# Perceiver block: the cross-partition maximum of the scores moves from TensorE transposes to one GpSimd instruction

## The chip, the cores and the metric

The kernel runs on one core of a Trainium2 chip. The metric is the device time of one execution in microseconds (us); lower is better. Engines are named as in the profile: PE (TensorE matmuls), PEld (its weight loads), DVE (VectorE), ACT (ScalarE), POOL (GpSimd), SP (the queue that issues the DMAs).

## The reference

A block of three residual layers over x of shape (8, 64, 256). The first, a cross attention with 16 heads of 64 over a context of 1601 rows, takes the larger part of the time:

```
xn = layernorm(layernorm(x), gamma, beta)
q  = xn @ w_q ; k, v = split(ctx @ w_kv)
scores = einsum('bqhd,bkhd->bhqk', q * SCALE, k)
attn = softmax(scores, axis=-1)
x = x + (einsum('bhqk,bkhd->bqhd', attn, v) @ w_out + b_out) * tanh(gate)
x = x + linear_attention(layernorm(x))     # 8 heads, 64 tokens
x = x + moe(layernorm(x))                  # 8 experts, top 2, all experts computed
```

The softmax here needs, for each query, the maximum of its scores over the 1601 context rows.

## The kernel before, in words

The weights of the keys are folded into the queries first, so that the scores are `ctx @ qk`, with qk computed once in a prologue, written to a DRAM scratch and read back. All large products are made in three passes of rounded operands: each operand is split into a high part (rounded to fp32r) and a low part (the rest), and hi*hi, hi*lo and lo*hi are summed.

The main loop has NSLOT = 208 slots: NG = 16 groups of SJ = 13 slots. A group is 512 columns (queries times heads of half a batch element), a slot is one piece of 128 context rows (65 rows in the thirteenth). Two groups share one batch element. Every engine has its own program, an unrolled walk over slots (a function `slot` in each), and the engines meet by semaphores. In slot k:

- PE computes the scores of slot k, context rows on the partitions (six matmuls, L1206), into one of two PSUM banks. It waits for `out_ok` and `max_ok` of slot k-2, since the bank must be free. Then it computes p times context of slot k-19 (`times_context`, twelve matmuls, L1224 to L1226).
- ACT copies the scores of slot k-1 out of PSUM (`take_scores`, L668), and takes the exponential and the high part of p of slot k-17 (`exps`, L674 and L677).
- DVE subtracts the maximum (`minus_max`, L882) of slot k-17, makes the low part of p (`low_part`, L907) of slot k-18, and keeps a running elementwise maximum `cmax` over the slots of the group (`running_max`, L890 and L893), in this order.

At the end of a group `cmax` holds 128 partial maxima for each of the 512 columns, and what is needed is their maximum, on every partition (`mbc`). That takes five steps on three engines: PE transposes `cmax` in four blocks (L1262, second slot of the next group), DVE reduces along the row and writes the result out 128 times wide (L899, L902, in `column_max`), PE transposes that back in four blocks (L1272, fourth slot), and ACT copies it to SBUF (L691, `take_max`). The first `minus_max` of the group waits for `mbc_ok`.

The context and qk pieces for later slots are split by POOL. `slot_jobs(k)` lists the pieces of slot k: one context piece for slot k+6 and in four of thirteen slots a piece of qk. Pieces are loaded by SP into a ring `raw` of four buffers (RR = 4); the load of piece n waits until piece n-4 is split (`split_ok`). POOL does both halves: the high part at L578, the low part at L580. In `may_split` it waits for the data and for the target: a score operand (ct) may be overwritten once `scores_ok` is far enough, a piece of the value operand (cn) once `pv_ok` is. Pieces of slots 7 to 19 of each 26 are of the cn kind.

In the sixth to tenth slot of a group (V_U to V_O) the finished sums of the group before are normalised (DVE L917), transposed (PE L1238), multiplied with w_v (PE L1251) and stored (L924). After slot 208 the loop drains while the linear attention of token tiles 0 to 2 (`chain`, with a POOL step `chain_rstd` at L603) starts between its slots. The experts follow.

The lines that the change touches: constants L51 and L54 to L55; buffers `mcol` L214 and `mrow` L252; POOL `split`, `split_job`, `split_pass` (L573 to L598); ACT `take_max` and `slot` (L688 to L712); DVE `column_max` (L895); PE `transpose_u` (L1229), `transpose_max` and `spread_max` (L1256 to L1273) and `slot`.

Of the kernel before, what the change touches and what calls it, by code (L numbers as in the profile page):

```python
# [34 lines left out]
P = 128  # L35
# [14 lines left out]
CNW = 2 * D + 2  # L50
L_SUB, L_LO, L_PV = SJ + 4, SJ + 5, SJ + 6  # L51
PASS = 4 * SJ
NPASS = NSLOT // PASS
V_MT, V_MR, V_MB, V_MC = 1, 2, 3, 3  # L54
V_U, V_UT, V_UTC, V_WV, V_O = 5, 6, 7, 8, 9  # L55
RR = 4
# [57 lines left out]
def build(nc, x, ctx_n, ctx_t, gamma, beta, w_q, w_kt, w_v, w_out, b_out, gate, Wq, Wk, Wv, Wo, bo,  # L114
          W_router, b_router, W1, b1, W2, b2, out):
    with ExitStack() as es:
# [96 lines left out]
        lnT_lo = sb("lnT_lo", [P, DT, TOK], F32R)  # L213
        mcol = sb("mcol", [P, GT])  # L214
        rsum = sb("rsum", [P, GT])
# [35 lines left out]
        pt_lo = lsb("pt_lo", [P, PR, GW], F32R)  # L251
        mrow = lsb("mrow", [P, GT, P])  # L252
        loop_scope.close()
# [32 lines left out]
        pool_step = sem("pool_step")  # L286
        split_hi = sem("split_hi")
        ones_ok = sem("ones_ok")
        split_ok = sem("split_ok")
# [16 lines left out]
        max_ok = sem("max_ok")  # L306
        mt_ok = sem("mt_ok")
        mcol_ok = sem("mcol_ok")
        mrow_ok = sem("mrow_ok")
        mb_ok = sem("mb_ok")  # L310
        mbc_ok = sem("mbc_ok")
# [238 lines left out]
        def _(pool):  # L550
# [21 lines left out]

            def split(src, hi, lo, hi_count, done):  # L573

                z = zero[0:src.shape[0], :]
                for _ in range(len(src.shape) - 2):
                    z = z.unsqueeze(1)
                pool.tensor_tensor(hi, src, z.broadcast_to(tuple(src.shape)), ALU.add).then_inc(split_hi, 1)  # L578
                pool.wait_ge(split_hi, hi_count + 1)
                pool.tensor_tensor(lo, src, hi.bitcast(F32), ALU.subtract).then_inc(done, 1)  # L580

            def split_job(job, i):

                no = linear(i, lambda q: JOB_NO[shift(job, q)])
                may_split(pool, job, i)
                split(*split_views(job, i), no, split_ok)

            def split_pass(i, of):
                for u in range(PASS):
                    for job in slot_jobs(of * PASS + u):  # L590
                        split_job(shift(job, -of), i)

            for job in FIRST_JOBS:
                split_job(job, 0)
            split_pass(0, 0)
            with pool.Fori(0, NPASS - 2) as i:
                split_pass(i, 1)
            split_pass(NPASS - 1, NPASS - 1)  # L598

            def chain_rstd(m, which):  # L600
# [25 lines left out]
        def _(act):  # L626
# [60 lines left out]

            def take_max(i, u):  # L688

                act.wait_ge(mb_ok, linear(i, lambda q: q * (PASS // SJ) + u // SJ))  # L690
                act.activation(mbc[:, (u // SJ - 1) % 2, :], wps[:, 1, :], ACT.Copy).then_inc(mbc_ok, 1)  # L691

            def slot(i, u, k):

                if 1 <= k <= NSLOT:
                    take_scores(i, u - 1)
                if u % SJ == V_MC and SJ <= k < NSLOT + SJ:
                    take_max(i, u)
                if L_SUB <= k < NSLOT + L_SUB:
                    exps(i, u - L_SUB)  # L700
                if u % SJ == V_UTC and k >= 2 * SJ:
                    take_ut(i, u)

            for u in range(PASS):
                slot(0, u, u)
                if u in LATE_TILE:
                    take_qk(LATE_TILE[u])
                if u - 1 in LATE_TILE:
                    first_high(LATE_TILE[u - 1])
            with act.Fori(0, NPASS - 1) as i:  # L710
                for u in range(PASS):
                    slot(i, u, PASS + u)  # L712
            def chain(m, o):

# [100 lines left out]
        def _(dve):  # L815
# [78 lines left out]

            def column_max(i, u):  # L895

                g = linear(i, lambda q: q * (PASS // SJ) + u // SJ)
                dve.wait_ge(mt_ok, g)
                dve.tensor_reduce(mcol[:], wps[:, 0, :].rearrange("p (t q) -> p t q", q=P), AX.X,  # L899
                                  ALU.max).then_inc(mcol_ok, 1)  # L900
                dve.wait_ge(mcol_ok, g)
                dve.tensor_copy(mrow[:], mcol[:].unsqueeze(2).broadcast_to((P, GT, P))).then_inc(mrow_ok, 1)  # L902

            def low_part(i, u):
# [22 lines left out]
            def slot(i, u, k):  # L927
                if L_SUB <= k < NSLOT + L_SUB:
                    minus_max(i, u - L_SUB)
                if L_LO <= k < NSLOT + L_LO:  # L930
                    low_part(i, u - L_LO)
                if 1 <= k <= NSLOT:
                    running_max(i, u - 1)
                if u % SJ == V_MR and SJ <= k < NSLOT + SJ:
                    column_max(i, u)
                if u % SJ == V_U and k >= 2 * SJ:
                    take_u(i, u)
                if u % SJ == V_O and k >= 2 * SJ:
                    b = u // (2 * SJ) - 1
                    if isinstance(i, int):  # L940
                        take_o(i, u, slice((i * 2 + b) * Q, (i * 2 + b + 1) * Q))
                    else:
                        take_o(i, u, bass.ds(i * (2 * Q) + (b + 2) * Q, Q))
# [198 lines left out]
        def _(pe):  # L1142
# [86 lines left out]
            def transpose_u(i, u):  # L1229
                for x in range(2):  # L1230
# [3 lines left out]
                    else:  # L1234
                        pe.wait_ge(mbc_ok, linear(i, lambda q: min(q * (PASS // SJ) + u // SJ, NG)))
                    for a in range(2):
# [18 lines left out]

            def transpose_max(i, u):  # L1256

                pe.wait_ge(max_ok, linear(i, lambda q: q * PASS + u // SJ * SJ))
                if not isinstance(i, int) or i > 0 or u >= 3 * SJ:
                    pe.wait_ge(o_ok, linear(i, lambda q: q * (PASS // SJ) + u // SJ - 2))  # L1260
                for t in range(GT):
                    ins = pe.transpose(wps[:, 0, t * P:(t + 1) * P],  # L1262
                                       cmax[:, (u // SJ - 1) % 2, t * P:(t + 1) * P], ident[:])
                ins.then_inc(mt_ok, 1)

            def spread_max(i, u):

                pe.wait_ge(mrow_ok, linear(i, lambda q: q * (PASS // SJ) + u // SJ))
                if not isinstance(i, int) or i > 0 or u >= 3 * SJ:
                    pe.wait_ge(utc_ok, linear(i, lambda q: (q * (PASS // SJ) + u // SJ - 2) * 2))  # L1270
                for t in range(GT):
                    ins = pe.transpose(wps[:, 1, t * P:(t + 1) * P], mrow[:, t, :], ident[:])  # L1272
                ins.then_inc(mb_ok, 1)  # L1273

            def slot(i, u, k):
                if k < NSLOT:
                    scores(i, u)
                if u % SJ == V_MT and SJ <= k < NSLOT + SJ:
                    transpose_max(i, u)
                if u % SJ == V_MB and SJ <= k < NSLOT + SJ:  # L1280
                    spread_max(i, u)
                if L_PV <= k < NSLOT + L_PV:
# [263 lines left out]
```

## Time and profile before

| | before |
|---|---|
| median of 3 runs | 981.15 us (978.63 to 981.46) |
| the profiled execution, time | 980.75 us |
| its span, first to last instruction | 979.0 us |
| PE busy | 936.0 us (96%) |
| DVE busy | 738.2 us (75%) |
| POOL busy | 561.9 us (57%) |
| ACT busy | 503.1 us (51%) |
| granted TensorE clock, mean | 0.991 |

Busy shares are averages over stages. Matmuls are pipelined and the profile models their ends, so that a PE matmul's duration is longer than the distance to the next one; distances between starts tell what an instruction costs. The loop runs from about 35 us to 737 us of the span.

### The profile page before, as it was taken

Reading aid. Unit: us, or ns where it says so; the run is one execution under the profiler, and the core shown is the slowest. Engines: PE = TensorE matmul, PEld = TensorE weight load, DVE = VectorE, ACT = ScalarE, POOL = GpSimd, SP = SyncE. Lnnn points to the kernel's source line nnn. Section 1 sums busy time; section 2 is a strip of 40 time slices with the busy share of each in tenths; the row PEclk is TensorE's granted clock in tenths of the full one; section 3 lists DMA queues with packets and bytes.
Section 4 is the critical chain, followed back from the end, with each engine's and each line's share of the span. In section 5 each row is a group of like instructions: output and inputs, shape, how many; then the busy total and the mean of one; then the engine's idle time right before and its main releaser. Section 6 shows DMA issues by size and latency. Waiting matters only on the chain.

```text
span 979.0 us, 18047 instructions
## 1 busy us (share of the span) xinstructions
PE 936.0 (96%) x5988; PEld 805.1 (82%) x5988; DVE 738.2 (75%) x1151; ACT 503.1 (51%) x856; POOL 561.9 (57%) x593
## 2 busy tenths in 40 slices
PE   6999999999999999999999999999998799999998
PEld 3568888888888888888889888888886587888887
DVE  4659778787877977878787797775875667888776
ACT  2557656566565665656646566564442333344332
POOL 5729779678948957967894895610010442444540
PEclk9999999999999999999999999999999799999999
DMA  5872122212211212221221221101005022222200
GB/s 161 271 253 55 51 60 63 53 45 62 63 38 58 66 36 60 62 52 46 60 67 30 58 70 37 51 1 65 1 1 172 5 84 86 87 86 86 86 1 22
DMA packets 75083, 66.40 MB, mean 68 GB/s; under 512 B 7920, under 2 KB 71680, under 8 KB 75008
## 3 DMA queue, kind: packets, MB, share of 16 engines
q1 hardware_dynamic: 75008, 65.37, 22.3%
q8 instruction: 51, 0.84, 0.3%
q14 instruction: 24, 0.20, 0.1%
HBM read 57.48 MB, written 7.86 MB: 67 GB/s over the span
## 4 chain that ended last, share of the span: by engine, by line
PE 85%; DVE 10%; ACT 2%; issue 2%; POOL 1%; DMA 0%; SPq 0%; DVEq 0%; ACTq 0%; POOLq 0%
PE sps L1206 27%; PE scp L1224 9%; PE scp L1226 9%; PE scp L1225 9%; PE scp L1416 5%; PE sps L1402 5%; PE wps L1402 4%; PE scp L1417 3%; DVE u_sb L917 2%; PE wps L1251 2%; DVE st L882 1%; PE sps L1160 1%; PE sps L1319 1%; PE scp L1174 1%; PE sps L1339 1%
## 5 line engine op out<-in xcount | busy, mean ns | idle before, releaser
L1224 PE MATMUL scp<-cn,pt_hi 128*128 128x258 f32 (+1 forms) x832 | 239.2, 288 | 3.6 <-DVE pt_lo L907 2.8
L1225 PE MATMUL scp<-cn,pt_hi 128*128 128x256 f32 (+1 forms) x832 | 234.9, 282 | 0.0
L1226 PE MATMUL scp<-cn,pt_lo 128*128 128x258 f32 (+1 forms) x832 | 234.8, 282 | 0.0
L907 DVE TENSOR_TENSOR pt_lo<-st,pt_hi 128x512 fp32r<-128x512 f32 (+1 forms) x208 | 196.6, 945 | 6.8 <-ACT pt_hi L677 6.8
L668 ACT ACTIVATE st<-sps 128x512 f32<-128x512 f32 (+1 forms) x208 | 123.6, 594 | 148.4 <-PE sps L1206 147.7
L882 DVE TENSOR_TENSOR st<-st,mbc 128x512 f32<-128x512 f32 (+1 forms) x208 | 158.9, 764 | 38.6 <-ACT mbc L691 38.0
L1206 PE MATMUL sps<-qk_hi,ct_hi 128*128 128x512 f32 (+1 forms) x416 | 168.3, 405 | 12.6 <-DVE cmax L893 5.6
L674 ACT ACTIVATE st<-st 128x512 f32<-128x512 f32 (+1 forms) x208 | 130.2, 626 | 88.7 <-DVE st L882 88.2
L1224 PEld LDWEIGHTS scp<-cn,pt_hi 128*128 128x128 f32 (+1 forms) x832 | 156.9, 189 | 13.7 <-DVE pt_lo L907 5.7
L1206 PE MATMUL sps<-qk_hi,ct_lo 128*128 128x512 f32 (+1 forms) x416 | 164.2, 395 | 0.0
L1206 PE MATMUL sps<-qk_lo,ct_hi 128*128 128x512 f32 (+1 forms) x416 | 163.4, 393 | 0.0
L1225 PEld LDWEIGHTS scp<-cn,pt_hi 128*128 128x128 f32 (+1 forms) x832 | 157.2, 189 | 7.4 <-issue 0.2
L1226 PEld LDWEIGHTS scp<-cn,pt_lo 128*128 128x128 f32 (+1 forms) x832 | 157.7, 190 | 0.0
L893 DVE TENSOR_TENSOR cmax<-cmax,sps 128x512 f32<-128x512 f32 x192 | 130.7, 681 | 33.9 <-ACT st L668 32.8
L578 POOL TENSOR_TENSOR cn<-raw,zero 128x256 fp32r<-128x256 f32 (+1 forms) x104 | 80.2, 772 | 120.4 <-PE scp L1226 113.9
L677 ACT ACTIVATE pt_hi<-st 128x512 fp32r<-128x512 f32 (+1 forms) x208 | 131.7, 633 | 7.5
L580 POOL TENSOR_TENSOR cn<-raw,cn 128x256 fp32r<-128x256 f32 (+1 forms) x104 | 100.3, 964 | 8.1
L1206 PEld LDWEIGHTS sps<-qk_hi,ct_hi 128*128 128x128 f32 (+1 forms) x416 | 76.5, 184 | 32.8 <-issue 14.2
L580 POOL TENSOR_TENSOR ct_lo<-raw,ct_hi 128x256 fp32r<-128x256 f32 (+1 forms) x104 | 96.0, 923 | 8.2
L578 POOL TENSOR_TENSOR ct_hi<-raw,zero 128x256 fp32r<-128x256 f32 (+1 forms) x104 | 88.3, 849 | 11.1 <-DMA raw<-ctx_t 11.1
L1206 PEld LDWEIGHTS sps<-qk_hi,ct_lo 128*128 128x128 f32 (+1 forms) x416 | 76.4, 184 | 20.3
L1206 PEld LDWEIGHTS sps<-qk_lo,ct_hi 128*128 128x128 f32 (+1 forms) x416 | 76.6, 184 | 10.3
(212 smaller groups left out, 1460.7 us busy)
## 6 DMA issues: line engine op xcount, KB each, us to landing
w_raw<-W SPq DMA_DIRECT2D x16, 1024.0 KB, 7.6
raw<-ctx_t SPq DMA_DIRECT2D x96, 128.0 KB, 2.2
raw<-ctx_n SPq DMA_DIRECT2D x96, 128.0 KB, 2.0
raw<-qk_scratch SPq DMA_DIRECT2D x56, 128.0 KB, 2.0
qk_scratch<-stage_b SPq DMA_DIRECT2D x4, 896.0 KB, 4.7
qk_scratch<-stage_a SPq DMA_DIRECT2D x4, 896.0 KB, 4.5
wq_sb<-w_q SPq DMA_DIRECT2D x1, 1024.0 KB, 5.0
wkt_sb<-w_kt SPq DMA_DIRECT2D x1, 1024.0 KB, 7.9
```

What stands on the lines that cost most here:

```text
L578: pool.tensor_tensor(hi, src, z.broadcast_to(tuple(src.shape)), ALU.add).then_inc(split_hi, 1)
L580: pool.tensor_tensor(lo, src, hi.bitcast(F32), ALU.subtract).then_inc(done, 1)
L668: act.activation(st[0:rows(j), par, j, :], sps[0:rows(j), u % 2, :], ACT.Copy).then_inc(out_ok, 1)
L674: act.activation(p, p, ACT.Exp).then_inc(exp_ok, 1)
L677: act.activation(pt_hi[0:rows(j), r, :], p, ACT.Copy).then_inc(hi_ok, 1)
L882: dve.tensor_tensor(p, p, mbc[0:rows(j), par, :], ALU.subtract).then_inc(sub_ok, 1)
L893: dve.tensor_tensor(m, m, src, ALU.max).then_inc(max_ok, 1)
L907: dve.tensor_tensor(pt_lo[0:rows(j), r, :], st[0:rows(j), par, j, :], pt_hi[0:rows(j), r, :].bitcast(F32), ALU.subtract).then_inc(lo_ok, 1)
L1206: ins = pe.matmul(sps[0:rows(j), u % 2, :], a[:, dt, cols], v[:, par, dt, :], start=c == 0, stop=c == 5)
L1224: pe.matmul(scp[:, t, 0:D + 2], hi, cn[0:rows(j), j, 0:D + 2], start=j == 0, stop=False)
L1225: pe.matmul(scp[:, t, 0:D], hi, cn[0:rows(j), j, D + 2:CNW], start=False, stop=False)
L1226: ins = pe.matmul(scp[:, t, 0:D + 2], lo, cn[0:rows(j), j, 0:D + 2], start=False, stop=j == SJ - 1)
```

## The change

Four edits that belong together:

1. POOL computes `mbc` from `cmax` by one `partition_all_reduce` with max for each group (`all_max`), with a small instruction ahead of it that carries the touch of `cmax`. It stands in POOL's program at the first slot of the next group, ahead of that slot's pieces, and after the last piece for the last group. The transposes on PE, `column_max` on DVE and `take_max` on ACT are gone.
2. In the loop ACT makes the high part of every piece (`high_part`, at the end of its slot k for the pieces of slot k), and POOL only the low part, after a wait for `slot_hi`. The 26 pieces ahead of the loop stay wholly with POOL.
3. L_SUB, L_LO and L_PV grow by one: `minus_max` is done for slot k-18, p times context for slot k-20. V_U to V_O move along by one, and so does the start of the last chain.
4. The second half of `transpose_u` waits for the copies of the group before (`utc_ok`), where it waited for `mbc_ok`.

```diff
-L_SUB, L_LO, L_PV = SJ + 4, SJ + 5, SJ + 6
+L_SUB, L_LO, L_PV = SJ + 5, SJ + 6, SJ + 7
-V_MT, V_MR, V_MB, V_MC = 1, 2, 3, 3
-V_U, V_UT, V_UTC, V_WV, V_O = 5, 6, 7, 8, 9
+V_U, V_UT, V_UTC, V_WV, V_O = 6, 7, 8, 9, 10
...
-            def split(src, hi, lo, hi_count, done):
+            def split(src, hi, lo, hi_count, done, both):
...
+                if both:
...
+                else:
+                    pool.wait_ge(slot_hi, hi_count + 1 - len(FIRST_JOBS))
                 pool.tensor_tensor(lo, src, hi.bitcast(F32), ALU.subtract).then_inc(done, 1)
...
+            def all_max(g, par):
+
+                pool.wait_ge(max_ok, (g + 1) * SJ)
+                pool.tensor_tensor(mtouch[:], cmax[:, par, 0:1], zero[:], ALU.add)
+                pool.partition_all_reduce(mbc[:, par, :], cmax[:, par, :], P, bass.bass_isa.ReduceOp.max)\
+                    .then_inc(mbc_ok, 1)
 
             def split_pass(i, of):
                 for u in range(PASS):
+                    if u % SJ == 0 and not (of == 0 and u == 0):
+                        all_max(linear(i, lambda q: q * (PASS // SJ) + u // SJ - 1), (u // SJ - 1) % 2)
                     for job in slot_jobs(of * PASS + u):
-                        split_job(shift(job, -of), i)
+                        split_job(shift(job, -of), i, False)
...
+            all_max(NG - 1, (NG - 1) % 2)
...
-            def take_max(i, u):
...
+            def high_part(job, i):
+
+                src, hi, _ = split_views(job, i)
+                may_split(act, job, i)
+                act.activation(hi, src, ACT.Copy).then_inc(slot_hi, 1)
+
+            def split_slot(i, of, u):
+
+                for job in slot_jobs(of * PASS + u):
+                    high_part(shift(job, -of), i)
...
             for u in range(PASS):
                 slot(0, u, u)
+                split_slot(0, 0, u)
...
-            def column_max(i, u):
...
-                        pe.wait_ge(mbc_ok, linear(i, lambda q: min(q * (PASS // SJ) + u // SJ, NG)))
+                        wait(pe, utc_ok, linear(i, lambda q: (q * (PASS // SJ) + u // SJ - 2) * 2))
...
-            def transpose_max(i, u):
...
-            def spread_max(i, u):
```

## Rows read from the trace of the kernel before

**Rows 1.** Page, busy time by engine, and the granted clock in 40 slices
```profile
PE 936.0 (96%) x5988; PEld 805.1 (82%) x5988; DVE 738.2 (75%) x1151; ACT 503.1 (51%) x856; POOL 561.9 (57%) x593
...
PEclk9999999999999999999999999999999799999999
```

**Rows 2.** Page, chain of work that ended last, share by engine
```profile
PE 85%; DVE 10%; ACT 2%; issue 2%; POOL 1%; DMA 0%; SPq 0%; DVEq 0%; ACTq 0%; POOLq 0%
```

**Rows 3.** Timeline of PE: start us, duration us, engine, line, operation, tiles
```profile
384.29 0.60 PE L1262 MATMUL wps<-ident,cmax 128*128 128x128 f32 x4
...
384.84 0.28 PE L1225 MATMUL scp<-cn,pt_hi 128*128 128x256 f32 x1
...
390.41 0.60 PE L1272 MATMUL wps<-ident,mrow 128*128 128x128 f32 x4
...
390.96 0.28 PE L1225 MATMUL scp<-cn,pt_hi 128*128 128x256 f32 x1
...
392.29 0.39 PE L1206 MATMUL sps<-qk_hi,ct_hi 128*128 128x512 f32 x1
...
393.67 0.28 PE L1224 MATMUL scp<-cn,pt_hi 128*128 128x258 f32 x1
393.79 0.28 PE L1225 MATMUL scp<-cn,pt_hi 128*128 128x256 f32 x1
...
395.10 0.40 PE L1206 MATMUL sps<-qk_hi,ct_hi 128*128 128x512 f32 x1
```

**Rows 4.** Groups by line: out<-in, shapes, count, busy us, mean ns, idle before
```profile
L899 DVE TENSOR_REDUCE mcol<-wps 128x4 f32<-128x512 f32 x16 | 10.9, 684 | 0.0
L1272 PE MATMUL wps<-ident,mrow 128*128 128x128 f32 x64 | 9.6, 272 | 0.7 <-DVE mrow L902 0.7
L691 ACT ACTIVATE mbc<-wps 128x512 f32<-128x512 f32 x16 | 9.6, 598 | 39.7 <-PE wps L1272 39.7
L674 ACT ACTIVATE st<-st 128x512 f32<-128x512 f32 (+1 forms) x208 | 130.2, 626 | 88.7 <-DVE st L882 88.2
L668 ACT ACTIVATE st<-sps 128x512 f32<-128x512 f32 (+1 forms) x208 | 123.6, 594 | 148.4 <-PE sps L1206 147.7
```

**Rows 5.** Timeline of PE in the filling of the loop
```profile
72.52 0.47 PE L1206 MATMUL sps<-qk_hi,ct_hi 128*128 128x512 f32 x1 [0.78 <-DVE cmax L893]
...
75.56 0.47 PE L1206 MATMUL sps<-qk_hi,ct_hi 128*128 128x512 f32 x1 [1.40 <-DVE cmax L893]
...
78.49 0.39 PE L1206 MATMUL sps<-qk_hi,ct_hi 128*128 128x512 f32 x1
```

**Rows 6.** Timeline of POOL, the first qk piece
```profile
72.76 0.70 POOL L578 TENSOR_TENSOR qk_hi<-raw,zero 128x256 fp32r<-128x256 f32 x1 [15.95 <-DMA raw<-qk_scratch]
```

**Rows 7.** Timeline of ACT, a rounding of a 128x256 piece
```profile
40.72 0.42 ACT L648 ACTIVATE qk_hi<-stage_b 128x256 fp32r<-128x256 f32 x1
```

**Rows 8.** Groups by line, POOL's elementwise work
```profile
L580 POOL TENSOR_TENSOR cn<-raw,cn 128x256 fp32r<-128x256 f32 (+1 forms) x104 | 100.3, 964 | 8.1
L609 POOL TENSOR_TENSOR w_lo<-w_raw,w_hi 128x1024 fp32r<-128x1024 f32 x16 | 40.5, 2536 | 70.0 <-ACT w_hi L763 70.0
```

**Rows 9.** Timeline of DVE around the end of a group
```profile
420.32 0.68 DVE L893 TENSOR_TENSOR cmax<-cmax,sps 65x512 f32<-65x512 f32 x1
...
432.61 0.69 DVE L882 TENSOR_TENSOR st<-st,mbc 128x512 f32<-128x512 f32 x1 [2.65 <-ACT mbc L691]
```

**Rows 10.** Timeline of PE, first score matmul after that group's end
```profile
420.94 0.39 PE L1206 MATMUL sps<-qk_hi,ct_hi 128*128 128x512 f32 x1
```

**Rows 11.** DMA issues: size and median us to landing
```profile
raw<-ctx_n SPq DMA_DIRECT2D x96, 128.0 KB, 2.0
```

**Rows 12.** Timeline of DVE, low part beside an idle and a busy POOL
```profile
394.88 0.68 DVE L907 TENSOR_TENSOR pt_lo<-st,pt_hi 128x512 fp32r<-128x512 f32 x1
...
400.72 1.17 DVE L907 TENSOR_TENSOR pt_lo<-st,pt_hi 128x512 fp32r<-128x512 f32 x1
```

**Rows 13.** Timeline of PE, the idle time after the transposes of u
```profile
402.63 0.47 PE L1206 MATMUL sps<-qk_hi,ct_hi 128*128 128x512 f32 x1 [0.81 <-ACT st L668]
```

More of the change, by code:

```diff
@@ L213, in build @@
         lnT_lo = sb("lnT_lo", [P, DT, TOK], F32R)
-        mcol = sb("mcol", [P, GT])
+        mtouch = sb("mtouch", [P, 1])
         rsum = sb("rsum", [P, GT])
@@ L251, in build @@
         pt_lo = lsb("pt_lo", [P, PR, GW], F32R)
-        mrow = lsb("mrow", [P, GT, P])
         loop_scope.close()
@@ L287, in build @@
         split_hi = sem("split_hi")
+        slot_hi = sem("slot_hi")
         ones_ok = sem("ones_ok")
@@ L306, in build @@
         max_ok = sem("max_ok")
[L307 to L310, printed above, removed]
         mbc_ok = sem("mbc_ok")
@@ L571, in _, with split_job @@
             pool.wait_ge(mask_ok, 1)
-            def split(src, hi, lo, hi_count, done):
[L575 to L579, printed above, removed]
+            def split(src, hi, lo, hi_count, done, both):
+                if both:
+                    z = zero[0:src.shape[0], :]
+                    for _ in range(len(src.shape) - 2):
+                        z = z.unsqueeze(1)
+                    pool.tensor_tensor(hi, src, z.broadcast_to(tuple(src.shape)), ALU.add).then_inc(split_hi, 1)
+                    pool.wait_ge(split_hi, hi_count + 1)
+                else:
+                    pool.wait_ge(slot_hi, hi_count + 1 - len(FIRST_JOBS))
                 pool.tensor_tensor(lo, src, hi.bitcast(F32), ALU.subtract).then_inc(done, 1)
-            def split_job(job, i):
+            def split_job(job, i, both):
                 no = linear(i, lambda q: JOB_NO[shift(job, q)])
-                may_split(pool, job, i)
-                split(*split_views(job, i), no, split_ok)
+                if both:
+                    may_split(pool, job, i)
+                split(*split_views(job, i), no, split_ok, both)
+            def all_max(g, par):
[3 more added lines that the diff above has]
+                    .then_inc(mbc_ok, 1)
             def split_pass(i, of):
                 for u in range(PASS):
+                    if u % SJ == 0 and not (of == 0 and u == 0):
+                        all_max(linear(i, lambda q: q * (PASS // SJ) + u // SJ - 1), (u // SJ - 1) % 2)
                     for job in slot_jobs(of * PASS + u):
-                        split_job(shift(job, -of), i)
+                        split_job(shift(job, -of), i, False)
             for job in FIRST_JOBS:
-                split_job(job, 0)
+                split_job(job, 0, True)
             split_pass(0, 0)
@@ L686, in take_ut @@
                                    wps[:, x, :].rearrange("p (a t q) -> p a t q", a=2, t=DT), ACT.Copy).then_inc(utc_ok, 1)
-            def take_max(i, u):
-                act.wait_ge(mb_ok, linear(i, lambda q: q * (PASS // SJ) + u // SJ))
-                act.activation(mbc[:, (u // SJ - 1) % 2, :], wps[:, 1, :], ACT.Copy).then_inc(mbc_ok, 1)
+            def high_part(job, i):
[5 more added lines that the diff above has]
+                    high_part(shift(job, -of), i)
             def slot(i, u, k):
@@ L696, in slot @@
                     take_scores(i, u - 1)
-                if u % SJ == V_MC and SJ <= k < NSLOT + SJ:
-                    take_max(i, u)
                 if L_SUB <= k < NSLOT + L_SUB:
@@ L709, in _ @@
                     first_high(LATE_TILE[u - 1])
-            with act.Fori(0, NPASS - 1) as i:
+            with act.Fori(0, NPASS - 2) as i:
                 for u in range(PASS):
                     slot(i, u, PASS + u)
+                    split_slot(i, 1, u)
+            for u in range(PASS):
+                slot(NPASS - 1, u, PASS * (NPASS - 1) + u)
+                split_slot(NPASS - 1, NPASS - 1, u)
             def chain(m, o):
@@ L893, in running_max @@
                     dve.tensor_tensor(m, m, src, ALU.max).then_inc(max_ok, 1)
-            def column_max(i, u):
[L897 to L902, printed above, removed]
             def low_part(i, u):
@@ L933, in slot @@
                     running_max(i, u - 1)
-                if u % SJ == V_MR and SJ <= k < NSLOT + SJ:
-                    column_max(i, u)
                 if u % SJ == V_U and k >= 2 * SJ:
@@ L1254, in times_wv @@
                 ins.then_inc(wv_ok, 1)
-            def transpose_max(i, u):
[L1258 to L1264, printed above, removed]
-            def spread_max(i, u):
[L1268 to L1273, printed above, removed]
             def slot(i, u, k):
@@ L1277, in slot @@
                     scores(i, u)
[L1278 to L1281, printed above, removed]
                 if L_PV <= k < NSLOT + L_PV:
```

## The prediction

> **What bounds the kernel now.** I read the page first: PE is busy 96% of the span at full clock [rows 1], and the chain of work that ended last runs over PE for 85% of it, over DVE for 10% and over POOL for 1% [rows 2]. So an instruction taken from PE is worth its whole distance, and one taken from DVE or ACT only where PE waited for it. The timeline of PE gives the beat: the scores of successive slots start at 392.29 and 395.10 us, so a slot is 2.81 us, and PE stands nowhere inside it [rows 3]. A group is 13 slots, 36.6 us, plus what PE does once per group.
>
> **What is removed.** Between the last score matmul and the second context matmul of an ordinary slot PE has 393.79 - 393.67 = 0.12 us from first to second; with the transposes of `cmax` it goes from 384.29 to 384.84, 0.55 us, and with those of `mrow` from 390.41 to 390.96, again 0.55 us [rows 3]. Each of the two is thus worth 0.43 us, and 16 groups have both: 32 x 0.43 = 13.8 us off PE. DVE loses its reduction of 0.68 us and the wide copy per group, and ACT 0.60 us [rows 4]. PE waited for that chain for 0.7 us only, once, in the drain [rows 4], so this counts as nothing: the cover is the slack between the ready `cmax` and the first `minus_max`.
>
> **What is moved.** ACT takes 182 context and 56 qk roundings at 0.42 us [rows 7], 100 us over 208 slots, 0.48 us a slot. Its slot was the copy of scores, 0.59, the exponential, 0.63 [rows 4], and a rounding taken as long as that, 1.85 us, and becomes 2.3 us against the beat of 2.81: no cost, as long as it does not wait. POOL's share per piece falls to the low part, 0.96 us [rows 8], 17 pieces in most groups, some 16 us of 40. No DMA is added, but SP's loads still wait for POOL's `split_ok` of four pieces earlier, and now ACT, in order, waits for those loads. What is queued behind ACT's wait is the next copy of scores, which DVE's running maximum and through it PE's scores two slots on need. Two costs come of that.
>
> The filling of the loop. The first qk piece is there at 72.76 us [rows 6], since SP first waits for the scratch and issues the weights. POOL alone waited before. Now ACT stands at the end of its slot 14 until then: rounding 0.42 [rows 7], copy of scores 14 0.59 [rows 4], running maximum 0.68 [rows 9], PE starts the scores of slot 16 at 74.5. Slots without a context product cost 1.6 us (1.39 of scores, and a bank that comes free late), so slot 20 starts at 80.9, against 78.49 [rows 5]: 2.4 us late. It started then with one context product done, 1.43 us, which is now still to do, and the 0.86 us of transposes are counted as gained above though they are inside the 78.49. The filling costs 2.4 + 1.4 + 0.9 = 4.7 us. The two idle times of 0.78 and 1.40 us there [rows 5] are in this balance.
>
> The steady loop is the size of the reduction against a deadline, below. The extra slot of latency gives DVE one more beat, and moves the drain by one slot, in which PE has the chains to work on: 0, within 1.5 us either way. In the drain the step at L603 is queued behind the last `all_max` on POOL; the first token tile's statistics come some 7 us after the last maximum, so up to that a reduction hides.
>
> **The price of the reduction, T.** No row shows one. From below: POOL's subtraction of 128x1024 takes 2.54 us [rows 8], so one pass over 128x512 is 1.27 us. From above: 128 partitions one after the other, 128 passes, 163 us. A tree of halvings has seven levels: one pass each is 8.9 us, a move and a maximum each 17.8 us. I take four passes, 5.1 us: nearest to the row, as the instruction reads once, folds, spreads and writes once, on an engine whose passes take all partitions together. This is the weak term of the sum.
>
> **The deadline.** Let slot 13 start at 0. After groups whose last slots carry ct pieces the maximum ends as now, at 420.32 + 0.68 = 421.00, beside a slot 13 starting at 420.94 [rows 9, 10]: at 0.1. In the other groups ACT rounds the cn pieces of slots 7 to 19, which are free only when the context product of the same slot is done, that is at the next slot's start; then 0.42 + 0.59 + 0.68 us make the maximum end at 1.7. POOL reduces until 1.7 + T and touches no piece meanwhile. The ring holds four pieces: those of slots 13, 14 (two) and 15. ACT's piece of slot 16 is loaded when POOL has done the piece of slot 13 (0.96 [rows 8]), with 2.0 us of DMA [rows 11]; then 0.42 rounding, 0.59 copy of scores 16, 0.68 maximum, and PE wants to start the scores of slot 18 at 5 x 2.81 = 14.1. So 1.7 + T + 0.96 + 2.0 + 0.42 + 0.59 + 0.68 <= 14.1: T up to 7.7 us is free after these eight groups and up to 9.3 after the other eight. `minus_max` itself allows more: it could wait now until 432.61, 11.6 us after the maximum [rows 9], and gets a beat more. Each us beyond costs 1 us per group.
>
> **Sum.** With T = 5.1: 980.75 - 13.8 + 4.7 = 971.7 us for the profiled execution. That execution lies 0.4 us under the median, so I forecast 972. Contention is set at nothing: the low part on DVE takes 0.68 us with POOL still and 1.17 with POOL working [rows 12], and the 0.81 us idle after the transposes of u [rows 13] (some eight such places, their causes on DVE and ACT) could shrink with POOL's second half gone: up to 5 us of gain. If the reduction itself disturbs DVE the same way, it takes the same back. Ends 966 and 976 for this case.
>
> [...]
>
> **The rivals.**
> 1. *The ring of four turns the reduction into a wait (slower).* Place: ACT's rounding in the fourth slot of a group, waiting for a load that waits for POOL. It decides from T = 7.7 us. With the seven levels of 8.9 us: 8 x 1.2 = 10 us back, 981. With 12 us: 8 x 4.3 + 8 x 2.7 = 56 less 9.1, 1028. With 17.8 us: 8 x 10.1 + 8 x 8.5 = 149 less 9.1, 1121. For it: POOL's rows are all slow beside DVE's, and nothing in the trace shows that it crosses partitions cheaply. Against: seven passes are needed before it costs anything. It equals no change at T of about 8.5 to 9.2.
> 2. *The reduction walks (much slower).* POOL folds partition by partition, 16 to 128 passes of 1.27 us, 20 to 163 us a group: 16 x (T - 8.5) less 9.1, from 1,156 to 3,440 us. For it: no row excludes it. Against: each elementwise row has all partitions at once. [...]
> 3. *The gain does not come out.* PE loses its transposes and waits instead for DVE at the same places, because ACT now delivers the scores up to 1.7 us later in half of the slots. For it: PE's waits name DVE and ACT [rows 5, 13]. Against: the running maximum of a cn slot ends 1.7 us after the next slot's start and is wanted at 2.81. It would give 978 to 984.
>
> **How the numbers follow.** Forecast case 0.52 (966 to 976). Rival 1 beyond no change 0.29, mostly 984 to 1121; rival 3, with the edge of rival 1, 0.07; rival 2 0.12. A measurement of this kernel can tell about 0.3%, 3 us, from no change. Faster: the forecast case and a little of the edge, 0.54; the same 0.05; slower 0.41. The range reaches down to 965 (all the contention gone) and up to 1055, where T is just under 14 us: at 14, 8 x 6.3 + 8 x 4.7 - 9.1 = 79 more, 1060. Above that lie the rest of rival 1 and rival 2, under 0.2 together. The forecast case has its own range, 966 to 976.
>
> **What would show it.** In the profile after: the mean duration of POOL's reduction in the groups by line, the one number on which all turns; PE 13 to 14 us less busy in the window of the loop; slots 14 to 16 of the filling with an idle time of about 5 us on PE, behind ACT; ACT at about 590 us busy. If the longest waits of ACT are those of the rounding for `raw` loads, one per group and each growing with T, rival 1 holds. If DVE's wait for `mbc` is the longest instead, my deadline is misplaced. The prediction is wrong if T is over 8 us, or if PE's loop keeps its length with T under 7.

## The result and the profile after

| | before | after |
|---|---|---|
| median | 981.17 us | 1107.74 us (1106.28 to 1109.88, 4 runs) |
| ratio, 95% interval | | 1.13 (1.1281 to 1.132) |
| the profiled execution, time | 980.75 us | 1109.88 us |
| its span | 979.0 us | 1108.1 us |
| granted TensorE clock, mean | 0.991 | 0.938 |

The change is 127 us slower. The forecast was 972 and the range ended at 1055. The page of the kernel after, busy time and clock, and the shares of the chain that ended last, which answer to [rows 1, 2]:

```profile
PE 963.0 (87%) x5860; PEld 824.0 (74%) x5860; DVE 671.3 (61%) x1119; ACT 562.9 (51%) x1078; POOL 349.2 (32%) x387
...
PEclk9989898998989899898989889898899998999999
...
PE 43%; issue 33%; POOL 10%; DVE 7%; DMA 2%; ACT 2%; SPq 1%; POOLq 0%; DVEq 0%; ACTq 0%
```

PE has its 128 transposes fewer and is still busy for 27 us longer, at 87% of the span; the granted clock has fallen, which is taken up below. No engine has taken over: POOL is at 32%. A third of the chain is "issue", time in which the engine waited for nothing that the profile shows. The chain of waits says where:

```profile
PE sps L1214 <- DVE cmax L912: 106.1, 31, 8.1
POOL mbc L591 <- issue: 101.1, 16, 10.5
...
ACT ct_hi L701 <- DMA raw<-ctx_t: 66.7, 7, 10.2
...
ACT cn L701 <- DMA raw<-ctx_n: 62.5, 7, 9.9
...
POOL ct_lo L578 <- issue: 49.0, 7, 7.5
POOL cn L578 <- issue: 48.6, 7, 7.1
```

PE waits for the running maximum, ACT waits for pieces in `raw` (14 times, 9 to 10 us, the last 6.6), and POOL stands 6.3 us on the mean ahead of each of 16 reductions and 7 us behind each. The timeline of POOL after one group shows one of them:

```profile
444.91 0.57 POOL L590 TENSOR_TENSOR mtouch<-cmax,zero 128x1 f32<-128x1 f32 x1 [0.56 <-DVE cmax L912]
451.31 1.80 POOL L591 PARTITION_ALL_REDUCE mbc<-cmax  x1 [5.82 <-issue]
459.86 1.31 POOL L578 TENSOR_TENSOR cn<-raw,cn 128x256 fp32r<-128x256 f32 x2 [6.75 <-issue]
```

And the queries on the two lines show what was issued there (count, shortest/median/longest ns, first and last start):

```profile
L591 POOLq MODIFY_POOL_CONFIG  x32: 3/6/8, 64.5 to 783.1; - x32
L591 POOL PARTITION_ALL_REDUCE mbc<-cmax x16: 1802/1842/2305, 75.0 to 790.2; - x16
...
L578 POOLq MODIFY_POOL_CONFIG  x30: 98/98/98, 76.7 to 744.6; - x30
```

The reduction itself is recorded at 1.84 us, far below the 5.1 us that the prediction took. But two MODIFY_POOL_CONFIG are issued ahead of each reduction, and two ahead of the first subtraction behind it. No line of the kernel asks for them. They stand where POOL goes from `tensor_tensor` to `partition_all_reduce` and where it goes back: 16 times there (x32) and 16 times back (x30, and x2 ahead of the step at L612 in the drain, at 792.2 us). I call such a pair a change of library, after the call `load_library`, which puts one into reload_pair below. The trace has a wait at every one of them: 5.82 us ahead of the reduction above, 5.8 to 6.2 us in the loop behind the first, which has 10.46, and 6.7 to 7.5 us behind a reduction. From the touch at 444.91 to the first low part at 459.86 POOL is away for 14.95 us, of which 1.8 us are the work. The rest of this text calls that the absence.

### The profile page after: what moved, and what is told of

It is laid out like the page before. It is cut to its first block, busy times and chain, and to the rows that moved or that the text cites. A ratio compares the mean times of both kernels' runs of the same rounds, so it can differ in the third digit from the quotient of the medians.

```text
span 1108.1 us, 17700 instructions
## 1 busy us (share of the span) xinstructions
PE 963.0 (87%) x5860; PEld 824.0 (74%) x5860; DVE 671.3 (61%) x1119; ACT 562.9 (51%) x1078; POOL 349.2 (32%) x387
## 4 chain that ended last, share of the span: by engine, by line
PE 43%; issue 33%; POOL 10%; DVE 7%; DMA 2%; ACT 2%; SPq 1%; POOLq 0%; DVEq 0%; ACTq 0%
PE sps L1214 10%; PE scp L1401 4%; PE wps L1387 4%; PE sps L1387 4%; PE scp L1232 3%; PE scp L1234 3%; PE scp L1233 3%; POOL ct_lo L578 3%; POOL cn L578 3%; PE scp L1402 2%; POOL qk_lo L578 2%; POOL mbc L591 2%; DVE cmax L912 1%; DVE u_sb L927 1%; ACT st L677 1%
## 5 line engine op out<-in xcount | busy, mean ns | idle before, releaser
L1214 PE MATMUL sps<-qk_hi,ct_hi 128*128 128x512 f32 (+1 forms) x416 | 179.6, 432 | 107.6 <-DVE cmax L912 106.1
L1232 PEld LDWEIGHTS scp<-cn,pt_hi 128*128 128x128 f32 (+1 forms) x832 | 164.5, 198 | 16.2 <-DVE pt_lo L917 5.7
L1214 PE MATMUL sps<-qk_hi,ct_lo 128*128 128x512 f32 (+1 forms) x416 | 172.1, 414 | 0.0
L1214 PE MATMUL sps<-qk_lo,ct_hi 128*128 128x512 f32 (+1 forms) x416 | 172.0, 414 | 0.0
L1233 PEld LDWEIGHTS scp<-cn,pt_hi 128*128 128x128 f32 (+1 forms) x832 | 164.2, 197 | 9.4 <-issue 0.5
L917 DVE TENSOR_TENSOR pt_lo<-st,pt_hi 128x512 fp32r<-128x512 f32 (+1 forms) x208 | 152.4, 733 | 1.5 <-ACT pt_hi L686 1.5
L901 DVE TENSOR_TENSOR st<-st,mbc 128x512 f32<-128x512 f32 (+1 forms) x208 | 150.7, 724 | 0.6 <-ACT tg L792 0.6
L578 POOL TENSOR_TENSOR cn<-raw,cn 128x256 fp32r<-128x256 f32 (+1 forms) x104 | 77.1, 744 | 223.3 <-ACT cn L701 173.7
L578 POOL TENSOR_TENSOR ct_lo<-raw,ct_hi 128x256 fp32r<-128x256 f32 (+1 forms) x104 | 85.4, 823 | 139.6 <-ACT ct_hi L701 89.5
L701 ACT ACTIVATE cn<-raw 128x256 fp32r<-128x256 f32 (+1 forms) x91 | 37.8, 415 | 127.8 <-PE scp L1234 65.3
L1401 PE MATMUL scp<-w_sp,h_hi 128*128 128x512 f32 x224 | 79.8, 397 | 1.0 <-DVE h_lo L1122 1.0
```

The source lines that it names most:

```text
L901: dve.tensor_tensor(p, p, mbc[0:rows(j), par, :], ALU.subtract).then_inc(sub_ok, 1)
L917: dve.tensor_tensor(pt_lo[0:rows(j), r, :], st[0:rows(j), par, j, :], pt_hi[0:rows(j), r, :].bitcast(F32), ALU.subtract).then_inc(lo_ok, 1)
L1214: ins = pe.matmul(sps[0:rows(j), u % 2, :], a[:, dt, cols], v[:, par, dt, :], start=c == 0, stop=c == 5)
L1232: pe.matmul(scp[:, t, 0:D + 2], hi, cn[0:rows(j), j, 0:D + 2], start=j == 0, stop=False)
L1233: pe.matmul(scp[:, t, 0:D], hi, cn[0:rows(j), j, D + 2:CNW], start=False, stop=False)
L1401: pe.matmul(scp[:, m, :], h_hi[:, f, ms], w2_sp[:, s, f, :], start=f == 0, stop=False)
```

## The experiments

The theory, A: the loss is POOL's absence, through the ring of four buffers, by the deadline of the prediction. The rivals: the reduction hides work that its record does not show (C); the rounding on ACT or the later slot cost much (B); the ring does not matter and only the first subtraction waits.

**One elementwise pass in place of the reduction.**

```diff
-                pool.tensor_tensor(mtouch[:], cmax[:, par, 0:1], zero[:], ALU.add)
-                pool.partition_all_reduce(mbc[:, par, :], cmax[:, par, :], P, bass.bass_isa.ReduceOp.max).then_inc(mbc_ok, 1)
+                pool.tensor_tensor(mbc[:, par, :], cmax[:, par, :], zero[:].broadcast_to((P, GW)), ALU.add).then_inc(mbc_ok, 1)
```

> The changed kernel with the reduction and its touch replaced by one elementwise POOL pass of 128x512 (maxima of each partition alone, so the output is not the reference's); nothing needs another POOL library. Theory A (the loss is POOL's absence of 15 us per group: a library load of 5.9 us, the reduction of 1.8 us, a load back of 6.8 us): with 1.3 us of absence all of it goes, and the sum of the prediction for a short reduction holds, 972 us (966 to 976). Rival B (the rounding on ACT and the later slot cost much by themselves): it stays above 990.

Measured: 968.14 us, ratio 0.9863 (0.9829 to 0.9898); the profiled execution 971.09 us, where the prediction's sum says 971.7. PE is busy 926.0 us of a span of 969.3. Its timeline in the filling of the loop has the one long wait:

```profile
73.89 0.77 PE L1212 MATMUL sps<-qk_hi,ct_hi 128*128 128x512 f32 x1 [5.86 <-DVE cmax L910]
```

All the other edits of the change are in this kernel, so B falls: together with the loss of the transposes they gain. The whole loss is in what was replaced. Its four runs are two pairs, 965.2 us at a granted clock of 0.994 and 971.1 to 971.3 us at 0.987 and 0.989; the median lies between them, so differences of medians against it are good to some 3 us.

**The changes of library without the reduction.** A call of `load_library` stands ahead of the same elementwise pass.

```diff
+                pool.load_library(library_config.all_libraries[1])
```

(behind the touch, ahead of the pass of one_pass)

> The changed kernel with the reduction replaced by one elementwise pass, and the two library loads kept ahead of it (the reduction is left out). Theory A: POOL is away for about 0.6 + 13 + 1.3 = 15 us as in the changed kernel, so 1095 to 1115 us though nothing is reduced across partitions. Rival C (the reduction itself, or work of it that the record of 1.8 us does not show, takes the time): below 1000.

Measured: 1098.73 us, ratio 1.1211 (1.1191 to 1.123), 131 us over one_pass, with nothing reduced. The queries on the line of the call, L592, and on that of the pass behind it, L593, have two MODIFY_POOL_CONFIG a group on each:

```profile
L592 POOLq MODIFY_POOL_CONFIG  x32: 4/6/8, 64.6 to 770.1; - x32
```

```profile
L593 POOLq MODIFY_POOL_CONFIG  x32: 7/7/7, 73.9 to 777.7; - x32
```

The timeline of its POOL after one group:

```profile
440.07 0.57 POOL L591 TENSOR_TENSOR mtouch<-cmax,zero 128x1 f32<-128x1 f32 x1 [0.56 <-DVE cmax L913]
453.56 1.03 POOL L593 TENSOR_TENSOR mbc<-cmax,zero 128x512 f32<-128x512 f32 x1 [12.92 <-issue]
```

And the timeline of its ACT behind it:

```profile
457.54 0.42 ACT L702 ACTIVATE cn<-raw 128x256 fp32r<-128x256 f32 x1 [8.61 <-DMA raw<-ctx_n]
```

A change there and back is 12.92 us of idle POOL, and T, from the touch to the first low part, 14.5 us. C falls: the 6.75 us behind the reduction in the kernel after belong to the change of library, not to a hidden tail.

**Is it the ring? Five, seven and ten passes.** The same pass repeated, each waiting for the one before, and no library change: POOL is away for as long as I choose.

```diff
+                pool.wait_ge(pass_ok, g * 9 + 1)
+                pool.tensor_tensor(mbc[:, par, :], cmax[:, par, :], zero[:].broadcast_to((P, GW)), ALU.add).then_inc(pass_ok, 1)
...
```

> As one_pass, with ten elementwise passes in a row, 12.5 us of POOL per group and no library load. If the deadline of the ring is right (7.7 us after half of the groups, 9.3 after the others): 8 x 4.8 + 8 x 3.2 = 64 us more than one_pass, about 1036. If instead only the first subtraction of the group sets the deadline (about 14.9 us after the maximum), the same as one_pass.

> As one_pass, with five passes in a row; a pass took 1.04 to 1.45 us from start to start in ten_passes, so POOL is away for 6 to 7 us per group. Deadline of the prediction (7.7 and 9.3 us): free, the same as one_pass, 968 (965 to 972). If the deadline lies lower than I reckon, it is over 975.

> As one_pass, with seven passes in a row, 9 to 10 us of POOL per group. Deadline of the prediction: at 10 us 8 x 2.3 + 8 x 0.7 = 24 us more than one_pass, 992 (at 9 us 978), and up to 20 us above that if PE's clock falls after each wait, as it did with ten passes. If only the first subtraction sets the deadline: 968.

The expected times were 968 us for five passes, 992 us for seven (up to 20 us more with the clock) and 1036 us for ten. The absence T is read on POOL's timeline, from the start of the first pass to the end of the last. Of seven passes:

```profile
444.94 1.42 POOL L591 TENSOR_TENSOR mbc<-cmax,zero 128x512 f32<-128x512 f32 x1 [1.16 <-DVE cmax L923]
...
453.68 1.97 POOL L603 TENSOR_TENSOR mbc<-cmax,zero 128x512 f32<-128x512 f32 x1
```

Of ten passes:

```profile
437.28 1.42 POOL L591 TENSOR_TENSOR mbc<-cmax,zero 128x512 f32<-128x512 f32 x1 [0.56 <-DVE cmax L929]
...
450.45 1.04 POOL L609 TENSOR_TENSOR mbc<-cmax,zero 128x512 f32<-128x512 f32 x1
```

| kernel | T, us | by the deadlines 7.7 and 9.3, over one_pass | measured median | over one_pass | PE's wait for `cmax` in all | PE busy |
|---|---|---|---|---|---|---|
| one_pass | 1.4 | 0 | 968.14 | | 12.1 | 926.0 |
| five_passes | 7.4 | 0 | 971.21 | 3 | 12.6 | 925.8 |
| seven_passes | 10.7 | 24 + 11 = 35 | 1011.73 | 44 | 39.8 | 934.9 |
| ten_passes | 14.2 | 52 + 39 = 91 | 1079.08 | 111 | 86.8 | 959.1 |
| reload_pair | 14.5 | 54 + 42 = 96 | 1098.73 | 131 | 95.2 | 959.9 |
| the change | 14.95 | 58 + 45 = 103 | 1107.74 | 140 | 106.1 | 963.0 |

Up to 7.4 us hardly anything happens; at 10.7 us the loss is 44 us. The rival that only the first subtraction matters (968 in every row) falls. PE's timeline shows the two deadlines one by one. The waits at 288.31 and 331.18 are of seven_passes, those at 215.46 and 360.08 of ten_passes, in each the wait behind a ct piece first, then that behind a cn piece:

```profile
288.31 0.47 PE L1225 MATMUL sps<-qk_hi,ct_hi 128*128 128x512 f32 x1 [1.36 <-DVE cmax L923]
331.18 0.47 PE L1225 MATMUL sps<-qk_hi,ct_hi 128*128 128x512 f32 x1 [3.27 <-DVE cmax L923]
```

```profile
215.46 0.77 PE L1231 MATMUL sps<-qk_hi,ct_hi 128*128 128x512 f32 x1 [4.87 <-DVE cmax L929]
360.08 0.76 PE L1231 MATMUL sps<-qk_hi,ct_hi 128*128 128x512 f32 x1 [6.70 <-DVE cmax L929]
```

With T = 10.7 the deadlines 9.3 and 7.7 give waits of 1.4 and 3.0 us; PE's are 1.3 to 1.5 and 3.0 to 3.3, six of each, in turn. With 14.2 they give 4.9 and 6.5; PE's are 4.3 to 4.9 and 6.4 to 6.7, apart from two of 3.4 late in the loop. But the ring makes PE wait behind 14 of the 16 groups only (behind 12 of them by more than 1 us with seven passes): the first falls into the filling, and behind the last no piece comes.

The expected time for seven passes was low because their T is 10.7 us and not the 9 to 10 that I wrote, and that for ten passes because theirs is 14.2 and not 12.5: in these loops a pass takes 1.37 to 1.97 us beside a working DVE, and 1.04 alone. The ratios are 0.989 (0.9865 to 0.9914), 1.0329 (1.0289 to 1.0368) and 1.0999 (1.098 to 1.1019).

The measured steps are 9, 20 and 37 us larger than the deadline gives for seven passes, ten passes and the change. PE's longer work at the lower clock makes the difference, while the waits alone are no more than the deadline gives. In the profiled executions the scores of slot 207, the last of the loop, start 42.3, 110.5 and 128.6 us later than in one_pass. 27.7, 74.7 and 94.0 us of this are waits for `cmax`. Up to that point PE runs the same matmuls, and is busy with them for 14.0, 35.6 and 35.4 us longer (641.8, 663.4 and 663.2 us against 627.8), at a mean granted clock of 0.98, 0.94 and 0.93 against 0.99. Behind the loop the change loses another 10.2 us, which the passes do not. 7.8 us of this are one wait in the drain, behind the last change of library:

```profile
POOL rstd L612 <- issue: 6.9, 1, 6.9
DVE ln_out L989 <- POOL rstd L612: 9.8, 2, 9.1
PE sps L1310 <- DVE ln_out L989: 7.8, 1, 7.8
```

In the kernel after, the timeline of PE around one wait:

```profile
455.42 0.39 PE L1214 MATMUL sps<-qk_hi,ct_lo 128*128 128x512 f32 x1
464.45 0.76 PE L1214 MATMUL sps<-qk_hi,ct_hi 128*128 128x512 f32 x1 [7.19 <-DVE cmax L912]
465.02 0.63 PE L1214 MATMUL sps<-qk_lo,ct_hi 128*128 128x512 f32 x1
465.44 0.63 PE L1214 MATMUL sps<-qk_hi,ct_lo 128*128 128x512 f32 x1
...
469.27 0.39 PE L1214 MATMUL sps<-qk_hi,ct_hi 128*128 128x512 f32 x1
469.51 0.39 PE L1214 MATMUL sps<-qk_lo,ct_hi 128*128 128x512 f32 x1
```

And the windows before, in and behind it (columns: window, length, busy us and instructions of PE, PEld, DVE, ACT, POOL, granted clock, DMA share, GB/s):

```profile
440.00:455.00 15.00, 15.00 (x97) 13.30 (x96) 10.99 (x17) 10.59 (x21) 3.75 (x4) 1.00 0.11 33
455.00:463.00 8.00, 2.27 (x16) 1.93 (x14) 0.00 (x0) 0.31 (x1) 2.67 (x4) 0.93 0.11 34
463.00:470.00 7.00, 5.54 (x22) 4.86 (x23) 3.95 (x6) 4.44 (x11) 2.29 (x3) 0.59 0.32 87
```

PE comes back slow from 7.19 us of idle: the matmuls of the scores start 0.43 us apart, and 0.24 us apart again by 469.27. The granted clock is 0.59 from 463 to 470 us; ahead of the wait, from 440 to 455, it was 1.00. Six matmuls of scores take 2.7 us in place of 1.4, and the twelve products behind them 2.1 in place of 1.4: 2.0 us for this wait, and 35.4 / 14 = 2.5 us on the mean.

**Edits 2 and 3 alone, on the kernel before.**

> The kernel before with edit 2 alone: ACT rounds the pieces of the loop, POOL makes the low parts; the maximum by transposes and the slot distances as before. Theory A: only the filling costs, 4.7 us less the 0.9 us of transposes that the sum had put in it, so 985; less some us if POOL's smaller share frees DVE. Rival B (ACT's waits for the context product of the same slot cost in every group): over 990.

> Edits 2 and 3 without the reduction: ACT rounds, and everything after the maximum is one slot later. Theory A: within 3 us of act_only, so 982 to 988. If the later slot costs one slot of products at the drain in full, 2.8 us more.

> The kernel before with edit 3 alone, every step after the maximum one slot later. Theory A: within 1.5 us of before, 980 to 983, as PE has the chains to do in the drain. Faster than before by 2 to 3 us if the extra beat removes idle times of PE behind DVE; act_and_later came out 3 us under act_only.

The first is edit 2 alone, the second edits 2 and 3, the third edit 3 alone, all with the transposes as before:

```diff
+            def split_slot(i, of, u):
+
+                for job in slot_jobs(of * PASS + u):
+                    high_part(shift(job, -of), i)
...
+                else:
+                    pool.wait_ge(slot_hi, hi_count + 1 - len(FIRST_JOBS))
```

```diff
-L_SUB, L_LO, L_PV = SJ + 4, SJ + 5, SJ + 6
+L_SUB, L_LO, L_PV = SJ + 5, SJ + 6, SJ + 7
...
-V_U, V_UT, V_UTC, V_WV, V_O = 5, 6, 7, 8, 9
+V_U, V_UT, V_UTC, V_WV, V_O = 6, 7, 8, 9, 10
```

Measured: act_only 984.7 us, ratio 1.003 (1.0018 to 1.0043); act_and_later 981.57 us, 1.0009 (0.9992 to 1.0026); later_only 978.0 us, 0.997 (0.9949 to 0.9991). The rounding on ACT costs 3.6 us. The extra slot lowers the median by 3.1 us in both places where it was added, where the theory gave 980 to 983 for later_only and 982 to 988 for act_and_later. It is not shown that the extra beat of DVE does this. At the same granted clock the gain is all but gone: later_only's profiled execution and that of before, both at 0.991, are 979.62 and 980.75, and act_and_later takes 984.4 to 986.0 at 0.987 and 0.988, where act_only has 982.8 to 985.0. What differs is how often a run has the higher clock: 0.991 or less in 3 of 10 runs of later_only and in 9 of 13 of before beside it. Why that is so stays open.

**Repair: no elementwise work for POOL in the loop.** The low parts go to DVE, one slot behind ACT's high parts; POOL has only the sixteen reductions in the loop, without the touch and written out so that their waits are constants.

```diff
+            def low_split(i, of, u):
+                for job in slot_jobs(of * PASS + u):
...
+                    dve.wait_ge(slot_hi, no)
+                    dve.tensor_tensor(lo, src, hi.bitcast(F32), ALU.subtract).then_inc(split_ok, 1)
```

> The changed kernel with the low parts of the pieces moved from POOL to DVE, so that POOL has nothing but the sixteen reductions in the loop and its library is loaded once. Theory A: POOL's reduction then takes 1.8 us and hides, and PE keeps the 13.8 us; DVE goes from 3 x 0.68 us a slot to that and 1.3 x 0.43 = 2.6 us, with 0.15 us a slot for the sums of a finished group, just under the beat of 2.81, so 970 to 985. If DVE becomes the bound it shows as PE idle behind cmax in every group: up to 1000.

Measured: 974.99 us, ratio 0.9949 (0.993 to 0.9969). The query on its reduction:

```profile
L590 POOL PARTITION_ALL_REDUCE mbc<-cmax x16: 1784/3092/3094, 64.9 to 659.8; - x16
L590 POOLq MODIFY_POOL_CONFIG  x2: 3/3/3, 56.7 to 56.8; - x2
```

Only one change of library is left for the sixteen reductions, ahead of the first, at 56.7 us, where POOL was idle anyway, and the loop is free of the 15 us. But the kernel is 6.8 us slower than one_pass: DVE has the low parts of 0.42 us each and is busy 727.7 us, against 673.7. PE's waits for the maximum, from the list of waits of one_pass, then of this kernel (total, times, longest):

```profile
PE sps L1212 <- DVE cmax L910: 12.1, 17, 5.9
```

```profile
PE sps L1230 <- DVE cmax L907: 16.8, 20, 6.2
```

Outside the filling the wait for the running maximum grows from 6.2 to 10.6 us; that this is the maximum standing behind the low parts in DVE's queue is the likely reason, and no run shows it alone. In exchange a low part of p takes 0.68 us on the mean [rows 12]. The profiled executions lie only 3.9 us apart, which these waits cover; the 6.8 us between the medians hold the scatter of both with the clock (low_on_dve ran from 972.2 us at 0.994 to 979.7 us at 0.987).

**Repair of the filling.** What makes ACT wait there is the first qk piece, which stands behind the issues of the weights in SP's queue. Here `load_pass` issues them eight slots later; their first use is after the loop.

```diff
-                    if of == 0 and u == SJ:
+                    if of == 0 and u == SJ + 8:
                         load_weights()
```

> low_on_dve with SP's ten loads of tail weights moved behind the first qk and context pieces (from slot 13 to slot 21). In low_on_dve PE stands 6.2 us in the filling behind ACT, which waits for the first qk piece. If that piece is late because SP issues the weights first, the stall goes and 5 to 6 us come back: 969 to 970. If the piece waits for the scratch itself, nothing changes: 975.

Measured: 969.25 us, ratio 0.986 (0.983 to 0.989), 5.7 us less, as expected. PE's longest wait in the filling, in its timeline, first in low_on_dve and then here:

```profile
74.58 0.76 PE L1230 MATMUL sps<-qk_hi,ct_hi 128*128 128x512 f32 x1 [6.16 <-DVE cmax L907]
```

```profile
76.01 0.47 PE L1231 MATMUL sps<-qk_hi,ct_hi 128*128 128x512 f32 x1 [1.57 <-DVE cmax L908]
```

On PE's timeline the scores of slot 39 start at 132.65 us in place of 140.53, 7.9 us earlier. Of this 3.8 us are left at the end of the profiled executions: from 655 to 800 us the granted clock is 0.94 here and 0.98 in low_on_dve. Of the three repaired kernels with the true maximum, this is the fastest: 11.9 us under the kernel before and 138 under the change.

**The extra slot once more.** The same kernel with edit 3 undone (`minus_max` back at k-17):

> low_dve_weights_later with edit 3 undone as well: the subtraction again 17 slots behind, the context product 19. The reduction lasts 1.8 to 3.1 us in low_on_dve, so its result is there before the subtraction one slot earlier wants it, and the pieces of the value operand come free one slot earlier for ACT. Theory A: the same or up to 2 us faster than low_dve_weights_later. Rival: DVE, at 2.7 us a slot, needs the extra beat, and it is 3 to 10 us slower.

Measured: 975.29 us, ratio 0.9944 (0.9925 to 0.9963), 6 us slower: the rival of the expectation holds and its theory does not. Here the slot of latency is worth 6 us, and the loop itself shows it: from the scores of slot 39 to those of slot 195 it takes 485.7 us against 479.5. PE's waits for `cmax` are 16.0 us against 10.7. On the kernel before, with DVE free of the low parts of the pieces, the same stretch gained 0.4 us by it (488.8 against 489.2).

## Why the prediction was wrong

**The step that failed is "The price of the reduction, T".** It asked what the instruction works, bounded the passes by rows and took 5.1 us. The work is 1.84 us, less than half. What counts is the time for which POOL is away, and that is 14.95 us: two changes of library a group, 5.8 us ahead and 6.75 behind, which reload_pair shows without any reduction (12.92 us, +131 us). The sum had no term for them. I did not ask what POOL runs between two reductions: subtractions, and in the trace of the kernel after each of the sixteen reductions, and what POOL runs first behind each, has its own two MODIFY_POOL_CONFIG and its own wait. No row of before could show it: its trace has no MODIFY_POOL_CONFIG but the two at 1.4 us. With T = 14.95 the prediction's own formula adds 8 x 7.25 + 8 x 5.65 = 103 us to 971.7: 1075, already outside the range, which stopped at a T of 14.

**The deadline was right**, and closely: waits of 3.0 to 3.3 and 1.3 to 1.5 us at T = 10.7, where 7.7 and 9.3 give 3.0 and 1.4. The mechanism is rival 1 as written, at its place: fourteen waits of ACT for `raw`, 9 to 10 us each and the last 6.6, where I had named "one per group and each growing with T". That is two groups fewer than the formula counts. The 103 us of the formula, 90 for fourteen groups, meet 101.8 us more of idle PE only because the 94.0 us of waits have the 7.8 us of the drain beside them. There the prediction let a reduction of up to 7 us hide ahead of the step at L603; POOL was away for longer than that.

**The price beyond the deadline was too low.** 1 us per us per group gives 91 of the 111 us of ten passes and 103 of 140 of the change. It leaves out that PE returns slow from 7.19 us of idle (0.59 granted over the next 7 us), 35.4 us in the loop of the change. The clock of [rows 1] is full but for one slice, and the sum had no term for it.

**The transposes: right.** From act_and_later (981.57) to one_pass (968.14) they and their chain go and one pass of POOL comes: 13.4 us, against 13.8 [rows 3]. What left DVE and ACT [rows 4] was rightly counted at next to nothing: from the scores of slot 39 to those of slot 195 the step is 11.2 us, and 12 x 0.86 = 10.3 of them are the transposes.

**The rest of the sum: two wrong terms that nearly cancel.** One_pass took 971.09 us where the sum says 971.7, and act_only 984.7 where 985 was expected. Both hits are in part luck: in one_pass the filling cost 2.5 us more than its term, and the loop 4.0 us less than the beat of before, as the starts of the scores of slots 39 and 195 show (PE's timeline, six score matmuls to a slot), before, then act_only, then one_pass:

```profile
135.61 0.39 PE L1206 MATMUL sps<-qk_hi,ct_hi 128*128 128x512 f32 x1
...
624.79 0.39 PE L1206 MATMUL sps<-qk_hi,ct_hi 128*128 128x512 f32 x1
```

```profile
143.38 0.39 PE L1228 MATMUL sps<-qk_hi,ct_hi 128*128 128x512 f32 x1
...
628.57 0.39 PE L1228 MATMUL sps<-qk_hi,ct_hi 128*128 128x512 f32 x1
```

```profile
139.63 0.39 PE L1212 MATMUL sps<-qk_hi,ct_hi 128*128 128x512 f32 x1
...
614.49 0.39 PE L1212 MATMUL sps<-qk_hi,ct_hi 128*128 128x512 f32 x1
```

**The filling: right in place, too small in size.** PE waits 5.86 us behind `cmax` where about 5 were expected, and the scores of slot 16 start at 73.89 (forecast 74.5). But at slot 39 act_only is 7.8 us late where 3.8 were reckoned. One_pass is 4.0 us late with two groups' transposes (1.7 us) gone and one product (1.4 us) still to do, so 7.2 us where the sum has 4.7. A part is the clock again: in one_pass the granted clock is 0.99 from 60 to 71 us and 0.53 from 71 to 78 us (in before 1.00 in both), and the scores of slots 16 and 17 take 2.7 and 1.9 us. The first qk piece behind the weights in SP's queue [rows 6] is the cause: with the weights later slot 39 starts 7.9 us earlier.

**ACT's rounding in the loop: not at nothing, but a gain.** From slot 39 to slot 195, twelve groups, before takes 489.2 us and act_only, with the same transposes, 485.2: 4.0 us less. One_pass takes 474.9, which is 14.3 less, and 10.3 of these are the transposes. The prediction had named this and set it at nothing: up to 5 us in PE's idle times like that of [rows 13], "with POOL's second half gone". They are gone in act_only (list of waits, before, then act_only):

```profile
PE sps L1206 <- ACT st L668: 4.9, 6, 0.8
```

```profile
PE sps L1228 <- ACT st L673: 0.9, 1, 0.9
```

ACT's roundings took 0.40 to 0.42 us as in [rows 7], but pieces in a row start 0.31 us apart; ACT was busy 562.9 us, not 590.

**The later slot: 0 within 1.5** fits the profiled execution, 1.1 us less at the same clock; the median of later_only is 3.2 us lower, with the open cause told above.

The low part of p falls from 0.95 us on the mean (median 1.10) to 0.73 after, and to 0.68 in low_on_dve [rows 12]. The query on the low part, before and after (shortest/median/longest ns):

```profile
L907 DVE TENSOR_TENSOR pt_lo<-st,pt_hi x208: 674/1097/1229, 74.1 to 734.5; 128x512 fp32r<-128x512 f32 x96, 65x512 fp32r<-65x512 f32 x8
```

```profile
L917 DVE TENSOR_TENSOR pt_lo<-st,pt_hi x208: 676/683/1606, 82.7 to 865.2; 128x512 fp32r<-128x512 f32 x96, 65x512 fp32r<-65x512 f32 x8
```

**The other rivals.** The walk (rival 2) falls: 1.84 us for 128 partitions. That the gain does not come out (rival 3, 978 to 984) falls with one_pass. Of the chances, the 0.29 of rival 1 held what happened, with T between its cases of 12 and 17.8 us (1028 and 1121).

## What to carry to other kernels

Before an instruction of GpSimd goes into a loop, look in a trace for MODIFY_POOL_CONFIG at it and at what GpSimd runs next: reductions and subtractions in turn cost 13 us a round here, seven times the 1.84 us of the instruction, and no busy share shows it (POOL 32%). Use such an instruction where GpSimd has nothing else in the loop, as in low_dve_weights_later (969.25 us). And count an engine's absence, not its work, against the deadline that its buffers set: below it hardly anything was lost here (3 us at T = 7.4), beyond it more than one to one (140 us where the deadlines give 103), since TensorE came back slow from its waits (0.59 granted). A total that comes out is no proof of its terms: the starts of the same slot in two kernels show in which stage each microsecond is won or lost.

## What the hardware showed that was not expected

- A change of library is 6.3 us of idle POOL on the mean ahead of `partition_all_reduce` (101.1 us in 16, the first of them 10.5) and 7.0 us behind it (97.6 us in 14); it stands in the profile only as MODIFY_POOL_CONFIG of 3 to 98 ns and idle time with the releaser "issue".
- `partition_all_reduce` of 128x512 is short, but took up to 3.09 us in low_on_dve, where only the first and the last of the sixteen took 1.8. A busy VectorE alone does not explain it: in the change the reduction at 451.31 took 1.80 us with DVE at work beside it, and there DVE's low part of p was the slower one, at 1.61 us. The cause is open. Timeline of POOL in low_on_dve:

```profile
64.94 1.81 POOL L590 PARTITION_ALL_REDUCE mbc<-cmax  x1 [8.17 <-DVE cmax L907]
...
301.20 3.09 POOL L590 PARTITION_ALL_REDUCE mbc<-cmax  x1 [38.36 <-DVE cmax L907]
```

- In the group of ten_passes that starts at 437.28 us the elementwise passes of POOL over 128x512 took 1.04 us with DVE at rest (from 448.21 us) and 1.37 to 1.97 us beside it. DVE's low part took 1.52 to 1.53 us beside them, but 0.68 beside the one of 1.97. In low_on_dve, where POOL has no elementwise work in the loop, all 208 took 0.68 to 0.69 us. The 0.68 us at 394.88 in [rows 12] is not beside a still POOL: in before POOL's rounding of a qk piece is recorded from 394.32 us for 1.71 us.
- After the 7.19 us of idle TensorE the granted clock was 0.59 on the mean over the next 7 us.
